# A GRU scan on one core: 1 - z moves from ScalarE to VectorE, the order of VectorE's step changes, and the scan's transfers go out once per tile

## The chip, the core and the metric

The kernel runs on one core of a Trainium2 chip (trn2). The metric is the device time of one execution in microseconds (us). A core has TensorE (PE, with its weight loads shown as PEld), VectorE (DVE), ScalarE (ACT), GpSimd (POOL) and SyncE (SP), which here only issues transfers. Each engine runs its own instructions strictly in the order in which they are written and waits for the others through semaphores.

## The reference

Inputs are x (16 x 256 x 512), a condition vector per batch (16 x 512), and weights. Two residual layers follow each other:

```
x = x + L0(x, cond)    # RMS norm, scale and shift from cond, 16-head attention over 256 positions, o + o @ W_out
x = x + L1(cond, x)    # GRU over the 256 positions; the first state is cond

# L1, one step, for each position in turn:
gi = x @ W_ih + b_ih ; gh = h @ W_hh + b_hh          # each 16 x 1536, split in r, z, n
r = sigmoid(i_r + h_r) ; z = sigmoid(i_z + h_z)
n = tanh(i_n + r * h_n)
h = (1 - z) * n + z * h                              # output of this position, state of the next
```

## The kernel before

The program has two stages. The first, up to about 772 us, computes the attention layer and the first two tiles of gi. The change does not touch it. The second is the scan: 256 steps, one after the other, since each needs the state h of the step before. A tile is ST = 8 steps, so there are 32 tiles.

The state h (16 x 512) is kept as 128 partitions x 128 columns: partition group j (32 partitions, 16 of them used) holds columns 128 j to 128 j + 127 of h. Every step is cut in two halves, q = 0 and q = 1, of 64 of these 128 columns. A half of a step is this chain, named by the functions of the code:

- TensorE multiplies the turned state hT by W_hh (line 632) into PSUM bank q, in which the gi part of the step already lies. The work of a step is 8 groups of 4 multiplications in the order (q, c) = (0,0), (0,1), (1,0), (0,2), (0,3), (1,1), (1,2), (1,3), with c a quarter of the sum over h. The profile counts two MATMUL rows for each, so a group is 8 rows and a step 64. Group (0,0) waits until half 0 of the new state is turned, (1,0) until bank 1 holds its gi part, and (0,2) until half 1 of the new state is turned, as c = 0 and 1 need half 0 of hT and c = 2 and 3 half 1.
- gates(q), line 1067, ACT: tanh for r and z once all four groups of half q are there. The kernel writes a sigmoid as (1 + tanh(a/2))/2.
- r_times_n(q), line 865, DVE: needs gates(q). Then before_n(q), line 870, DVE, and tanh_n(q), line 1075, ACT.
- one_less_z(q), line 1071, ACT: 1 - z out of gates(q). z_times_h(q), line 874, DVE: z times the old state. Both are needed after tanh_n(q).
- new_part(q), line 880, DVE: needs tanh_n(q). new_h(q), line 884, DVE. turn_h(q), line 891, DVE: the 32 x 32 block transpose that makes hT for the next step.
- seed(q), line 1084, ACT: copies the gi part of the next step into PSUM bank q.

Behind the multiplications of a step TensorE runs 4 or 5 of the 36 pieces (line 604, 128 x 512 columns each) that compute gi of a tile two tiles ahead; `START` spreads them evenly over steps 0 to 239, so 120 steps have 4, 120 have 5, and the last 16 have none. Once per tile, 29 times in steps 0 to 239 and each time in a step of 4 pieces, TensorE also turns a block of x (line 502). The results pass through nat (line 738, DVE) into DRAM (gscr, line 288) and come back laid out for the scan in a buffer GI (lines 277 and 282), two of which alternate. POOL adds the residual (line 1184, s_og counts steps) into outG, which SP stores (line 360). SP walks through the steps as well: before the change it waits for s_og at each step and issues one to three of the transfers.

Of the kernel before, what the change touches and what calls it, by code (L numbers as in the profile page):

```python
# [8 lines left out]
ALU = mybir.AluOpType  # L9
ACT = mybir.ActivationFunctionType  # L10
# [8 lines left out]
ST = 8  # L19
NT = T // ST  # L20
# [51 lines left out]
def cond_resid_kernel(nc, x, cond, W_emb, b_emb, g_norm, W_qkv, g_q, g_k, W_out, W_ih, W_hh, b_ih, b_hh, out):  # L72
# [3 lines left out]
    with ExitStack() as ctx:  # L76
# [29 lines left out]
        bias = sb("bias", [128, 3 * D])  # L106
# [67 lines left out]
        GI = [GI0, GI1]  # L174
# [67 lines left out]
        def _(sp):  # L242
# [27 lines left out]

            def gi_free(tt):

                sp.wait_ge(s_og, ST * (tt - 1))
                sp.wait_ge(s_h, 2 * ST * (tt - 1))

            def load_gx(tt, j):
                sp.dma_start(GI[tt % 2][32 * j:32 * j + 16, :, 4, :], x_j[tt, j]).then_inc(s_gl[tt % 2], 16)

            def load_gates(tt, j):
                v = gscr[tt].rearrange("(s b) j g f -> j b s (g f)", s=ST)  # L280
                sp.wait_ge(s_st[tt % 2], 48 * (tt // 2 + 1))
                sp.dma_start(GI[tt % 2][32 * j:32 * j + 16, :, 1:4, :].rearrange("p s g f -> p s (g f)"),
                             v[j]).then_inc(s_gl[tt % 2], 16)

# [52 lines left out]
            load_x1(1)  # L337
            sp.wait_ge(s_bz, 9)
            for j in range(4):
                load_gx(0, j)  # L340
            load_x1(2)
            store_x1(NB - 1, 1)
            for g in range(3):
                store_gate(0, g)
            for j in range(4):
                load_gates(0, j)
            load_x1(3)
            for g in range(3):
                store_gate(1, g)
            sp.wait_ge(s_bz, 17)  # L350
            for j in range(4):
                load_gx(1, j)
                load_gates(1, j)
            load_x1(4)

            o_v = out.rearrange("b (t s) (j f) -> t j b s f", s=ST, j=4)

            def store_h(tt, j):
                sp.wait_ge(s_og, ST * (tt + 1))
                sp.dma_start(o_v[tt, j], outG[32 * j:32 * j + 16, tt % 2, :, :]).then_inc(s_out[tt % 2], 16)  # L360

            for t in range(T):
                tt, s = t // ST, t % ST

                if tt:
                    sp.wait_ge(s_og, t)
                    if s < 4:
                        store_h(tt - 1, s)
                    if tt + 1 < NT:
                        if s == 0:  # L370
                            gi_free(tt + 1)
                        if s < 2:
                            load_gx(tt + 1, 2 * s)
                            load_gx(tt + 1, 2 * s + 1)
                        elif s < 6:
                            load_gates(tt + 1, s - 2)
                for pt, g, k, turn in pieces(t):
                    if turn and pt + 3 < NT:
                        load_x1(pt + 3)
                    if k == GP - 1:  # L380
                        store_gate(pt, g)
            for j in range(4):
                store_h(NT - 1, j)
            for e in range(2):
# [258 lines left out]
        def _(v):  # L643
# [214 lines left out]
            for t in range(T):  # L858
# [4 lines left out]
                def r_times_n(q):  # L863
                    v.wait_ge(s_tr, 2 * t + q + 1)
                    v.scalar_tensor_tensor(out=v_v[:, q, :], in0=v_rz[:, q, 0:64], scalar=1.0, in1=ps[:, q, 0:64],  # L865
                                           op0=ALU.add, op1=ALU.mult).then_inc(s_u, 1)

                def before_n(q):
                    v.wait_ge(s_u, 2 * t + q + 1)
                    v.scalar_tensor_tensor(out=v_w[:, q, :], in0=v_v[:, q, :], scalar=0.5, in1=gi[:, f[q]],  # L870
                                           op0=ALU.mult, op1=ALU.add).then_inc(s_w, 1)

                def z_times_h(q):
                    v.scalar_tensor_tensor(out=v_h[:, q, :], in0=v_rz[:, q, 64:128], scalar=1.0, in1=h_old[:, f[q]],
                                           op0=ALU.add, op1=ALU.mult)

                def new_part(q):

                    v.wait_ge(s_n, 2 * t + q + 1)
                    v.tensor_tensor(v_n[:, q, :], v_n[:, q, :], v_c[:, q, :], ALU.mult).then_inc(s_d, 1)  # L880
# [11 lines left out]

                r_times_n(0)
                before_n(0)
                if t >= 2:
                    v.wait_ge(s_og, t - 1)
                z_times_h(0)
                new_part(0)
                r_times_n(1)
                new_h(0)  # L900
                before_n(1)
                turn_h(0)
                z_times_h(1)
# [10 lines left out]
        def _(s):  # L914
# [149 lines left out]
            for t in range(T):  # L1064
# [3 lines left out]

                def one_less_z(q):
                    s.wait_ge(s_tr, 2 * t + q + 1)  # L1070
                    s.activation(v_c[:, q, :], v_rz[:, q, 64:128], ACT.Copy, bias=0.5, scale=-0.5)  # L1071

                def tanh_n(q):
# [13 lines left out]
                gates(0)  # L1087
                one_less_z(0)
                tanh_n(0)
                gates(1)  # L1090
                seed(0)
                one_less_z(1)
                tanh_n(1)
# [119 lines left out]
```

## Time and profile before

| | us |
|---|---|
| median of 3 runs (lowest, highest) | 1822.72 (1821.93, 1822.9) |
| the profiled execution: its own time | 1821.93 |
| its span, first to last instruction | 1820.1 |
| PE busy | 1755.0 (96%) |
| DVE busy | 1191.0 (65%) |
| ACT busy | 1008.7 (55%) |
| POOL busy | 409.4 (22%) |

Some 1.8 us of the profiled execution lie outside the span. The share of busy time is a mean over both stages and does not say which engine sets the time of a step; the rows of single steps do. In such rows the first number is the start in us from the span's start, the second the duration, and a number in brackets is how long the engine had been idle.

### The profile page before, as it was taken

The page shows a single profiled execution, that of the slowest core. Times are in us where ns is not written, and L with a number is a line of the kernel's source. Part 1 is how long each engine was busy: PE and PEld are TensorE (multiplying, and loading weights), DVE is VectorE, ACT ScalarE, POOL GpSimd, SP SyncE. Part 2 cuts the span into 40 slices and gives each one's busy share as a digit, 9 for nine tenths or more (in the row PEclk, how much of TensorE's full clock was granted, in tenths as well). Part 3 has the DMA queues.
Part 4 walks back from the last instruction along what each step waited for, and adds up shares of the span by engine and source line. Part 5 has one row for each costly group of instructions (what it writes and reads, how often), then busy time and mean ns, then how long its engine had stood idle before and what let it go on. Part 6 is the DMA issues. An engine that isn't in the chain of part 4 may idle for free.

```text
span 1820.1 us, 59314 instructions
## 1 busy us (share of the span) xinstructions
PE 1755.0 (96%) x23849; PEld 1293.7 (71%) x23849; DVE 1191.0 (65%) x4508; ACT 1008.7 (55%) x3691; POOL 409.4 (22%) x481
## 2 busy tenths in 40 slices
PE   6999999999999998799999999999999999999986
PEld 4677777777777776577777777777777777777765
DVE  5777777777777777355666666666665666666554
ACT  4777777777777776144444444444444444444444
POOL 5533333333433432111111111111111111111111
PEclk8999999999999999899999999999999999999999
DMA  5021111111111111743332332323323233232220
GB/s 214 23 96 42 42 36 36 36 36 36 36 36 36 36 36 35 157 71 75 78 79 70 75 75 76 79 72 73 76 76 76 74 72 77 74 78 69 64 68 14
DMA packets 130490, 118.80 MB, mean 65 GB/s; under 512 B 9932, under 2 KB 108440, under 8 KB 130216
## 3 DMA queue, kind: packets, MB, share of 16 engines
q1 hardware_dynamic: 130216, 115.00, 24.1%
q8 instruction: 190, 3.11, 0.8%
q14 instruction: 84, 0.69, 0.1%
HBM read 73.01 MB, written 41.94 MB: 63 GB/s over the span
## 4 chain that ended last, share of the span: by engine, by line
PE 93%; DMA 2%; ACT 2%; DVE 1%; issue 1%; POOL 1%; SPq 0%; POOLq 0%; DVEq 0%
PE ps L632 38%; PE ps L604 17%; PE ps L422 13%; PE ps L461 7%; PE ps L492 5%; PE ps L448 4%; PE ps L475 4%; PE ps L430 2%; PE ps L404 1%; PE ps L502 1%; PE ps L482 1%; DMA xscr<-x1s 1%; ACT qT L955 1%; ACT P L969 0%; DMA wemb<-in_L_cond_W_emb_dram 0%
## 5 line engine op out<-in xcount | busy, mean ns | idle before, releaser
L632 PE MATMUL ps<-whh,hT 128*32 128x192 f32 x16384 | 719.0, 327 | 20.9 <-DVE hT L891 17.4
L632 PEld LDWEIGHTS ps<-whh,hT 128*32 128x32 f32 x16384 | 546.4, 110 | 194.2 <-issue 84.9
L1067 ACT ACTIVATE v<-ps 128x128 f32<-128x128 f32 x512 | 139.1, 272 | 441.5 <-PE ps L632 441.5
L1184 POOL TENSOR_TENSOR outG<-hG,GI 128x128 f32<-128x128 f32 x256 | 117.1, 457 | 959.9 <-DVE hG L884 959.9
L865 DVE SCALAR_TENSOR_TENSOR v<-v,ps 128x64 f32<-128x64 f32 x512 | 113.4, 222 | 316.6 <-ACT v L1067 316.6
L969 ACT ACTIVATE P<-ps,nmx 128x256 f32<-128x256 f32 x512 | 242.4, 489 | 0.7 <-DVE nmx L690 0.7
L1075 ACT ACTIVATE v<-v 128x64 f32<-128x64 f32 x512 | 131.4, 257 | 107.1 <-DVE v L870 107.1
L1123 POOL TENSOR_TENSOR rq<-msq,mh 128x16 f32<-128x16 f32 x64 | 187.1, 2923 | 5.3
L690 DVE TENSOR_REDUCE nmx<-ps 128x2 f32<-128x512 f32 x256 | 164.9, 686 | 29.8 <-PE ps L448 28.0
L422 PE MATMUL ps<-wqh,xh 128*128 128x512 f32 x384 | 165.5, 431 | 4.7 <-POOL xl L1114 4.6
L604 PE MATMUL ps<-wih_h,x1h 128*128 128x512 f32 x384 | 166.6, 434 | 1.4 <-DVE x1l L729 1.4
L604 PE MATMUL ps<-wih_h,x1l 128*128 128x512 f32 x384 | 164.3, 428 | 0.0
L1084 ACT COPY ps<-GI 128x192 f32<-128x192 f32 x510 | 163.2, 320 | 0.0
L880 DVE TENSOR_TENSOR v<-v,v 128x64 f32<-128x64 f32 x512 | 115.5, 226 | 63.7 <-ACT v L1075 47.9
L422 PE MATMUL ps<-wql,xh 128*128 128x512 f32 x384 | 152.9, 398 | 0.0
L422 PE MATMUL ps<-wqh,xl 128*128 128x512 f32 x384 | 151.4, 394 | 0.0
L604 PE MATMUL ps<-wih_l,x1h 128*128 128x512 f32 x384 | 151.4, 394 | 0.0
L1034 ACT COPY PT<-ps 128x512 f32<-128x512 f32 x128 | 75.1, 586 | 125.8 <-PE ps L461 125.7
L461 PE MATMUL ps<-ident,P 128*128 128x128 f32 x1024 | 140.3, 280 | 1.8 <-DVE rTs L695 1.3
L461 PEld LDWEIGHTS ps<-ident,P 128*128 128x128 f32 x1024 | 109.8, 141 | 44.7 <-issue 42.1
L1071 ACT ACTIVATE v<-v 128x64 f32<-128x64 f32 x512 | 130.7, 255 | 8.1
L891 DVE STREAM_TRANSPOSE hT<-hG 128x64 f32<-128x64 f32 x510 | 123.4, 242 | 8.8
(104 smaller groups left out, 2449.3 us busy)
## 6 DMA issues: line engine op xcount, KB each, us to landing
gscr<-nat SPq DMA_DIRECT2D x96, 256.0 KB, 2.6
GI<-gscr SPq DMA_DIRECT2D x128, 192.0 KB, 3.7
xb<-in_x_dram SPq DMA_DIRECT2D x16, 512.0 KB, 3.7
xres<-in_x_dram SPq DMA_DIRECT2D x32, 256.0 KB, 2.8
xscr<-x1s SPq DMA_DIRECT2D x32, 256.0 KB, 2.0
x1n<-xscr SPq DMA_DIRECT2D x32, 256.0 KB, 2.7
GI<-xscr SPq DMA_DIRECT2D x128, 64.0 KB, 2.7
out_dram<-outG SPq DMA_DIRECT2D x128, 64.0 KB, 2.9
```

The lines of the kernel that those rows point to most:

```text
L422: last = pe.matmul(pB, xp[:, c, m], wp[:, c, n], start=(c == 0 and k == 0), stop=(c == KC - 1 and k == 2))
L461: last = pe.transpose(pP[:, j, k, :], P[:, U % 2, j, 128 * k:128 * k + 128], ident)
L604: last = pe.matmul(F[G % 2], xp[:, tt % 2, c, :], wp[:, c, g * D:(g + 1) * D], start=(k == 0), stop=(k == GP - 1), skip_group_check=True)
L632: last = pe.matmul(ps[32 * j:32 * j + 32, q, 0:192], hT[:, 32 * c:32 * c + 32], whg[:, c, :, 128 * j + 64 * q:128 * j + 64 * q + 64], star ...
L690: v.tensor_reduce(nmx[:, U % 2, 2 * h:2 * h + 2], pS2[h], AXX, ALU.max, negate=True).then_inc(s_mx, 1)
L891: v.transpose(hT[:, f[q]], h_new[:, f[q]]).then_inc(s_hc, 1)
L969: last = s.activation(P[:, U % 2, j, :], pS[j], ACT.Exp, bias=nmx[:, U % 2, j:j + 1], accum_out=rsum[:, U % 2, j:j + 1])
L1067: s.activation(v_rz[:, q, :], ps[:, q, 64:192], ACT.Tanh, scale=0.5).then_inc(s_tr, 1)
L1071: s.activation(v_c[:, q, :], v_rz[:, q, 64:128], ACT.Copy, bias=0.5, scale=-0.5)
L1075: s.activation(v_n[:, q, :], v_w[:, q, :], ACT.Tanh).then_inc(s_n, 1)
L1084: s.copy(ps[:, q, 0:192].rearrange("p (g f) -> p g f", g=3), GI[(t + 1) // ST % 2][:, (t + 1) % ST, 0:3, 64 * q:64 * q + 64]).then_inc(s_s ...
L1123: g_.tensor_tensor(rq[:, i, :], msq[:, i, :], mh, ALU.pow).then_inc(s_rq, 1)
```

## The change

Three things change.

- one_less_z(q) leaves ACT (an activation with scale and bias) and becomes a tensor_scalar on DVE. ACT's wait in front of it goes with it.
- The order of DVE's step changes. Before: r_times_n(1) stands between new_part(0) and new_h(0), and before_n(1) ahead of turn_h(0). After: new_h(0) stands ahead of r_times_n(1), turn_h(0) follows, and one_less_z(1) and before_n(1) come behind turn_h(0). The wait for s_og (POOL's residual of two steps ago) moves from z_times_h(0) to one_less_z(0).
- SP no longer waits for s_og at every step. At the last step of a tile it waits once, issues the four stores of the tile at once, and behind them the four loads of x and the four of the gates for the tile two further on.

The core of the diff, DVE and ACT:

```diff
+                def one_less_z(q):
+                    v.tensor_scalar(v_c[:, q, :], v_rz[:, q, 64:128], -0.5, 0.5, ALU.mult, ALU.add)
...
                 r_times_n(0)
-                before_n(0)
                 if t >= 2:
                     v.wait_ge(s_og, t - 1)
+                one_less_z(0)
+                before_n(0)
                 z_times_h(0)
                 new_part(0)
+                new_h(0)
                 r_times_n(1)
-                new_h(0)
+                turn_h(0)
+                one_less_z(1)
                 before_n(1)
-                turn_h(0)
                 z_times_h(1)
                 new_part(1)
                 new_h(1)
...
-                def one_less_z(q):
-                    s.wait_ge(s_tr, 2 * t + q + 1)
-                    s.activation(v_c[:, q, :], v_rz[:, q, 64:128], ACT.Copy, bias=0.5, scale=-0.5)
...
                 gates(0)
-                one_less_z(0)
                 tanh_n(0)
                 gates(1)
                 seed(0)
-                one_less_z(1)
                 tanh_n(1)
                 seed(1)
```

SP:

```diff
+            def load_gx(tt):
+                x1_there(tt)
+                sp.wait_ge(s_bz, (9, 17)[tt % 2])
+                if tt >= 2:
+                    sp.wait_ge(s_og, ST * (tt - 1))
+                    sp.wait_ge(s_h, 2 * ST * (tt - 1))
+                for j in range(4):
+                    sp.dma_start(GI[tt % 2][32 * j:32 * j + 16, :, 4, :], x_j[tt, j]).then_inc(s_gl[tt % 2], 16)
+
+            def load_g(tt):
                 v = gscr[tt].rearrange("(s b) j g f -> j b s (g f)", s=ST)
+                if tt:
+                    load_gx(tt)
                 sp.wait_ge(s_st[tt % 2], 48 * (tt // 2 + 1))
-                sp.dma_start(GI[tt % 2][32 * j:32 * j + 16, :, 1:4, :].rearrange("p s g f -> p s (g f)"),
-                             v[j]).then_inc(s_gl[tt % 2], 16)
+                for j in range(4):
+                    sp.dma_start(GI[tt % 2][32 * j:32 * j + 16, :, 1:4, :].rearrange("p s g f -> p s (g f)"),
+                                 v[j]).then_inc(s_gl[tt % 2], 16)
...
-                if tt:
-                    sp.wait_ge(s_og, t)
-                    if s < 4:
-                        store_h(tt - 1, s)
-                    if tt + 1 < NT:
-                        if s == 0:
-                            gi_free(tt + 1)
-                        if s < 2:
-                            load_gx(tt + 1, 2 * s)
-                            load_gx(tt + 1, 2 * s + 1)
-                        elif s < 6:
-                            load_gates(tt + 1, s - 2)
                 for pt, g, k, turn in pieces(t):
                     if turn and pt + 3 < NT:
                         load_x1(pt + 3)
                     if k == GP - 1:
                         store_gate(pt, g)
+                        if g == 2:
+                            stored = pt
+                            if t > ST * (pt - 1) - 1:
+                                load_g(pt)
+                if s == ST - 1:
+                    sp.wait_ge(s_og, t + 1)
+                    for j in range(4):
+                        sp.dma_start(o_v[tt, j], outG[32 * j:32 * j + 16, tt % 2, :, :]).then_inc(s_out[tt % 2], 16)
+                    if tt + 2 <= stored:
+                        load_g(tt + 2)
```

The instructions as they stand in the built programs follow. Line numbers of the changed program are its own: there r_times_n is L854, one_less_z L858, before_n L862, z_times_h L866, new_part L871, new_h L875 and turn_h L882. In the names v_113 is the buffer of tanh(r) and tanh(z), v_114 of r times n, v_115 of tanh_n's input, v_116 of n, v_117 of 1 - z and v_118 of z times h.

DVE in the scan, one whole step of the kernel before, from r_times_n(0) to turn_h(1):

```order
L865 SCALAR_TENSOR_TENSOR v_114<-v_113,ps 128x64
L870 SCALAR_TENSOR_TENSOR v_115<-v_114,GI_104 128x64
L874 SCALAR_TENSOR_TENSOR v_118<-v_113,hG 128x64
L880 TENSOR_TENSOR v_116<-v_116,v_117 128x64
L865 SCALAR_TENSOR_TENSOR v_114<-v_113,ps 128x64
L884 SCALAR_TENSOR_TENSOR hG<-v_118,v_116 128x64
L870 SCALAR_TENSOR_TENSOR v_115<-v_114,GI_104 128x64
L891 STREAM_TRANSPOSE hT<-hG 128x64
L874 SCALAR_TENSOR_TENSOR v_118<-v_113,hG 128x64
L880 TENSOR_TENSOR v_116<-v_116,v_117 128x64
L884 SCALAR_TENSOR_TENSOR hG<-v_118,v_116 128x64
L891 STREAM_TRANSPOSE hT<-hG 128x64
```

DVE, the first 12 of the 14 instructions of one step of the changed kernel, from r_times_n(0) to new_part(1) (new_h(1) and turn_h(1) follow):

```order
L854 SCALAR_TENSOR_TENSOR v_114<-v_113,ps 128x64
L858 TENSOR_SCALAR v_117<-v_113 128x64
L862 SCALAR_TENSOR_TENSOR v_115<-v_114,GI_107 128x64
L866 SCALAR_TENSOR_TENSOR v_118<-v_113,hG 128x64
L871 TENSOR_TENSOR v_116<-v_116,v_117 128x64
L875 SCALAR_TENSOR_TENSOR hG<-v_118,v_116 128x64
L854 SCALAR_TENSOR_TENSOR v_114<-v_113,ps 128x64
L882 STREAM_TRANSPOSE hT<-hG 128x64
L858 TENSOR_SCALAR v_117<-v_113 128x64
L862 SCALAR_TENSOR_TENSOR v_115<-v_114,GI_107 128x64
L866 SCALAR_TENSOR_TENSOR v_118<-v_113,hG 128x64
L871 TENSOR_TENSOR v_116<-v_116,v_117 128x64
```

The second SCALAR_TENSOR_TENSOR that reads ps, r_times_n(1), has moved from ahead of new_h(0) to behind it, and between it and before_n(1) now stand the transpose and the TENSOR_SCALAR.

ACT in one step of the kernel before (L1067 gates, L1071 one_less_z, L1075 tanh_n, L1084 seed), from gates(0) to seed(1):

```order
L1067 ACTIVATE v_113<-ps 128x128
L1071 ACTIVATE v_117<-v_113 128x64
L1075 ACTIVATE v_116<-v_115 128x64
L1067 ACTIVATE v_113<-ps 128x128
L1084 COPY ps<-GI_104 128x192
L1071 ACTIVATE v_117<-v_113 128x64
L1075 ACTIVATE v_116<-v_115 128x64
L1084 COPY ps<-GI_104 128x192
```

ACT in one step of the changed kernel (L1060 gates, L1064 tanh_n, L1073 seed):

```order
L1060 ACTIVATE v_113<-ps 128x128
L1064 ACTIVATE v_116<-v_115 128x64
L1060 ACTIVATE v_113<-ps 128x128
L1073 COPY ps<-GI_104 128x192
L1064 ACTIVATE v_116<-v_115 128x64
L1073 COPY ps<-GI_104 128x192
```

The two ACTIVATE into v_117 are gone and the rest keeps its order.

SP in the scan of the kernel before, from the store of one gate of a tile to the loads of the next tile's GI (L288 gscr, L269 x, L360 output, L277 and L282 GI):

```order
L269 DMA x1n_105<-xscr 128x512
L288 DMA gscr<-nat_111 512x1x128
L360 DMA out_dram<-outG 16x8x128
L277 DMA GI_107<-xscr 16x8x128 x2
L360 DMA out_dram<-outG 16x8x128
L277 DMA GI_107<-xscr 16x8x128 x2
L360 DMA out_dram<-outG 16x8x128
L282 DMA GI_107<-gscr 16x8x384
L288 DMA gscr<-nat_110 512x1x128
L360 DMA out_dram<-outG 16x8x128
```

SP of the changed kernel (L292 gscr, L269 x, L370 output, L278 and L286 GI), from one tile's gate loads to the next tile's:

```order
L269 DMA x1n_121<-xscr 128x512
L292 DMA gscr<-nat_110 512x1x128
L370 DMA out_dram<-outG 16x8x128 x4
L278 DMA GI_104<-xscr 16x8x128 x4
L286 DMA GI_104<-gscr 16x8x384 x4
L292 DMA gscr<-nat_111 512x1x128 x2
L269 DMA x1n_105<-xscr 128x512
```

Transfers that stood one or two at a time between stores of the gates now stand as a block of 4, 4 and 4 once per tile.

## Rows read from the trace of the kernel before

**Rows 1.** Stretches: us, PE, PEld, DVE, ACT, POOL busy, granted clock, DMA share, GB/s

```profile
1500.00:1752.00 252.00, 251.07 (x4267) 182.06 (x4263) 154.87 (x775) 118.00 (x503) 28.18 (x62) 1.00 0.29 72
1755.00:1811.00 56.00, 39.59 (x904) 33.35 (x908) 31.21 (x172) 26.08 (x114) 6.39 (x14) 1.00 0.14 30
```

**Rows 2.** Timeline (start, duration, engine, line, operation), the first step's r_times_n(0)

```profile
774.91 0.22 DVE L865 SCALAR_TENSOR_TENSOR v<-v,ps 128x64 f32<-128x64 f32 x1 [2.94 <-ACT v L1067]
```

**Rows 3.** Timeline, r_times_n(0) of the last step

```profile
1812.91 0.22 DVE L865 SCALAR_TENSOR_TENSOR v<-v,ps 128x64 f32<-128x64 f32 x1 [1.41 <-ACT v L1067]
```

**Rows 4.** Waits from 1755 to 1811 us: total, times, longest

```profile
PE ps L632 <- DVE hT L891: 17.4, 15, 1.2
```

**Rows 5.** Timeline of one step without pieces (last: idle before, releaser)

```profile
1769.30 0.22 DVE L865 SCALAR_TENSOR_TENSOR v<-v,ps 128x64 f32<-128x64 f32 x1 [1.42 <-ACT v L1067]
...
1769.55 0.23 DVE L870 SCALAR_TENSOR_TENSOR v<-v,GI 128x64 f32<-128x64 f32 x1
1769.69 0.22 DVE L874 SCALAR_TENSOR_TENSOR v<-v,hG 128x64 f32<-128x64 f32 x1
...
1770.10 0.23 DVE L880 TENSOR_TENSOR v<-v,v 128x64 f32<-128x64 f32 x1 [0.19 <-ACT v L1075]
...
1770.27 0.22 DVE L865 SCALAR_TENSOR_TENSOR v<-v,ps 128x64 f32<-128x64 f32 x1
1770.38 0.25 ACT L1071 ACTIVATE v<-v 128x64 f32<-128x64 f32 x1
1770.41 0.22 DVE L884 SCALAR_TENSOR_TENSOR hG<-v,v 128x64 f32<-128x64 f32 x1
1770.54 0.22 DVE L870 SCALAR_TENSOR_TENSOR v<-v,GI 128x64 f32<-128x64 f32 x1
1770.68 0.24 DVE L891 STREAM_TRANSPOSE hT<-hG 128x64 f32<-128x64 f32 x1
1770.84 0.18 DVE L874 SCALAR_TENSOR_TENSOR v<-v,hG 128x64 f32<-128x64 f32 x1
1770.96 0.31 ACT L1084 COPY ps<-GI 128x192 f32<-128x192 f32 x1
...
1771.06 0.37 PE L632 MATMUL ps<-whh,hT 128*32 128x192 f32 x4 [1.16 <-DVE hT L891]
```

**Rows 6.** Timeline, a step with 5 pieces

```profile
1203.19 0.22 DVE L865 SCALAR_TENSOR_TENSOR v<-v,ps 128x64 f32<-128x64 f32 x1 [1.41 <-ACT v L1067]
...
1205.09 2.81 PE L632 MATMUL ps<-whh,hT 128*32 128x192 f32 x64
```

**Rows 7.** The page's groups: count, busy us, mean ns, idle before

```profile
L632 PE MATMUL ps<-whh,hT 128*32 128x192 f32 x16384 | 719.0, 327 | 20.9 <-DVE hT L891 17.4
```

**Rows 8.** Timeline, the step that also turns a block of x

```profile
1027.76 0.22 DVE L865 SCALAR_TENSOR_TENSOR v<-v,ps 128x64 f32<-128x64 f32 x1 [0.97 <-ACT v L1067]
...
1029.86 2.32 PE L632 MATMUL ps<-whh,hT 128*32 128x192 f32 x52
```

**Rows 9.** Timeline, DVE's end of the step of rows 5

```profile
1771.08 0.23 DVE L880 TENSOR_TENSOR v<-v,v 128x64 f32<-128x64 f32 x1
1771.34 0.22 DVE L884 SCALAR_TENSOR_TENSOR hG<-v,v 128x64 f32<-128x64 f32 x1
1771.60 0.24 DVE L891 STREAM_TRANSPOSE hT<-hG 128x64 f32<-128x64 f32 x1
```

**Rows 10.** One line's instructions: count, duration ns min/median/max, starts

```profile
L759 DVE TENSOR_SCALAR gqs<-vT x1: 144/144/144, 16.8 to 16.8; 128x1 f32<-128x1 f32 x1
```

**Rows 11.** Another line's instructions, columns as in rows 10

```profile
L647 DVE TENSOR_SCALAR xb<-xb,rx x32: 476/479/486, 13.0 to 645.3; 128x512 f32<-128x512 f32 x32
```

**Rows 12.** SP's timeline, the loads of one tile's GI

```profile
1199.65 0.88 SPq L277 DMA_DIRECT2D GI<-xscr  x2
...
1212.66 5.87 SPq L282 DMA_DIRECT2D GI<-gscr  x3
```

**Rows 13.** Chain of waits at the scan's start: start, us, what

```profile
764.53 7.28 DMA GI<-gscr
```

More of the change, by code:

```diff
@@ L269, in load_x1 @@
                 sp.dma_start(x1n[tt % 2], x_v[tt]).then_inc(s_xl[tt % 2], 16)
[L271 to L279, printed above, removed]
+            def load_gx(tt):
[7 more added lines that the diff above has]
+            def load_g(tt):
                 v = gscr[tt].rearrange("(s b) j g f -> j b s (g f)", s=ST)
+                if tt:
+                    load_gx(tt)
                 sp.wait_ge(s_st[tt % 2], 48 * (tt // 2 + 1))
-                sp.dma_start(GI[tt % 2][32 * j:32 * j + 16, :, 1:4, :].rearrange("p s g f -> p s (g f)"),
-                             v[j]).then_inc(s_gl[tt % 2], 16)
+                for j in range(4):
+                    sp.dma_start(GI[tt % 2][32 * j:32 * j + 16, :, 1:4, :].rearrange("p s g f -> p s (g f)"),
+                                 v[j]).then_inc(s_gl[tt % 2], 16)
             def store_gate(tt, g):
@@ L337, in _ @@
             load_x1(1)
-            sp.wait_ge(s_bz, 9)
-            for j in range(4):
-                load_gx(0, j)
+            load_gx(0)
             load_x1(2)
@@ L344, in _ @@
                 store_gate(0, g)
-            for j in range(4):
-                load_gates(0, j)
+            load_g(0)
             load_x1(3)
@@ L349, in _ @@
                 store_gate(1, g)
[L350 to L353, printed above, removed]
+            load_g(1)
             load_x1(4)
             o_v = out.rearrange("b (t s) (j f) -> t j b s f", s=ST, j=4)
-            def store_h(tt, j):
-                sp.wait_ge(s_og, ST * (tt + 1))
-                sp.dma_start(o_v[tt, j], outG[32 * j:32 * j + 16, tt % 2, :, :]).then_inc(s_out[tt % 2], 16)
+            stored = 0
             for t in range(T):
                 tt, s = t // ST, t % ST
-                if tt:
-                    sp.wait_ge(s_og, t)
-                    if s < 4:
-                        store_h(tt - 1, s)
-                    if tt + 1 < NT:
-                        if s == 0:
-                            gi_free(tt + 1)
-                        if s < 2:
-                            load_gx(tt + 1, 2 * s)
-                            load_gx(tt + 1, 2 * s + 1)
-                        elif s < 6:
-                            load_gates(tt + 1, s - 2)
                 for pt, g, k, turn in pieces(t):
@@ L381, in _ @@
                         store_gate(pt, g)
-            for j in range(4):
-                store_h(NT - 1, j)
+                        if g == 2:
[8 more added lines that the diff above has]
+                        load_g(tt + 2)
             for e in range(2):
```

## The prediction, as it was made before the changed kernel had run

> **What bounds the kernel now.** The busy shares point at TensorE (96% of the span), and a busy TensorE is easily taken for the limit. So I went first to the table of stretches: from 1500 to 1752 us, while TensorE also works on gi, it is busy 251.07 of 252 us; from 1755 to 1811 us, without that work, 39.59 of 56 us, at the same granted clock of 1.00 (the 2.4 GHz level) [rows 1]. Next I wanted the length of a step in both. I measure it from r_times_n(0) to r_times_n(0), and call that moment of each step 0. Over the whole scan it is (1812.91 - 774.91) / 255 = 4.071 us [rows 2, 3]. In the bare steps the waits say what ends last: TensorE waits 15 times for turn_h, 17.4 us in all, so 1.16 each [rows 4]. The timeline of one such step [rows 5] shows turn_h(0) starting at 1.38 (1770.68 - 1769.30) and TensorE's group (0,0) at 1.76.
>
> How long is a bare step? The group spacing follows from the merged row of 64 multiplications in 2.81 us [rows 6]: one of them runs 0.33 us [rows 7], and a half group (four at once) takes half the spacing, so with s the spacing 2.81 = 8 s - s/2 + 0.33, and s = 0.33 us. That puts (0,2) three groups behind (0,0): 1.76 + 0.98 = 2.74. The bare step is 17.4 / 15 = 1.16 us of waiting plus the 2.81 us run = 3.97 us, so the next 0 comes 3.97 - 2.74 = 1.23 behind the start of (0,2). With a piece count of 5, (0,0) starts at 1205.09 - 1203.19 = 1.90 [rows 6] and in the 29 steps that also turn a block of x at 1029.86 - 1027.76 = 2.10 [rows 8]: by the same 2.21 from (0,0) to the next 0 these take 4.11 and 4.31 us. The sum closes: 1038.0 less 120 x 4.11 and 29 x 4.31 leaves 419.8 for the other 106 intervals, 3.96 each, the bare step's length, so the steps of 4 pieces are set by the chain of the state too. So TensorE's own work costs at most 0.34 us over the bare chain of half 0, and the chain of the state is almost as long as TensorE's work everywhere.
>
> The number that matters most is the slack of half 1. turn_h(1) starts at 1771.60 - 1769.30 = 2.30 [rows 9], and TensorE starts 0.38 after a transpose starts (1770.68 to 1771.06, [rows 5]): hT is ready for (0,2) at 2.68. It is wanted at 2.74. Half 1 is late if it loses more than 0.06 us in a bare step, 0.20 in one of 5 pieces and 0.40 in the turning one.
>
> **The order on VectorE, step by step.** All from [rows 5, 9]. A dependent instruction starts 0.25 to 0.26 behind its predecessor's start (L865 to L870, L880 to L884, L884 to L891), an independent one 0.13 to 0.14 behind it (L870 to L874, L865 to L884, L884 to L870), and one behind the transpose 0.16. From before_n to new_part, with tanh_n on ScalarE between, it is 0.55 in half 0 and 0.54 in half 1. What the rows do not have is the new TENSOR_SCALAR on 64 columns. From above, its slot is that of L874, 0.14, or at the far end the 0.22 of a whole such record, as if nothing overlapped. From below, 0, as if the engine took no turn for it. I take 0.11: a TENSOR_SCALAR of one column took 144 ns [rows 10] and one of 512 columns 479 [rows 11], which by a straight line makes 144 + 63/511 x 335 = 185 ns for 64, about 0.04 less than the 0.22 us of the two-input ones, so 0.14 - 0.04 = 0.10, and I round up.
>
> The Trainium skill's "VectorE: DVE Perf Modes", section "The perf-mode tier table (the rule you actually need)", says that a tensor_scalar from SBUF to SBUF runs fp32 at two elements a cycle while a tensor_tensor stays at one. By it the slot would be an estimated 0.14 - 32/960 = 0.107 us, and the sum the same; no row here has this form at this size.
>
> Half 0 after: r_times_n(0) 0; one_less_z(0) 0.14; before_n(0) at 0.25 (0.14 + 0.11, and it waits until 0.25 anyway, so nothing is lost); new_part(0) 0.80; new_h(0) 1.06, where r_times_n(1) no longer stands ahead of it; r_times_n(1) 1.19; turn_h(0) 1.33. Half 0 gains 0.05: group (0,0) could start at 1.71 instead of 1.76.
>
> Half 1 after: r_times_n(1) 1.19, against 0.97 before (1770.27), since it now stands behind new_h(0), and its engine waits there for tanh_n(0). Then it has to let two more pass: the transpose at 1.33, one_less_z(1) at 1.49, before_n(1) at 1.60 (before 1.24, so 0.36 later); new_part(1) 2.14; new_h(1) 2.40; turn_h(1) 2.66. hT is ready at 2.66 + 0.38 = 3.04, where the old schedule wants it at 2.74. The next 0 comes at 3.04 + 1.23 = 4.27 us.
>
> The other edits on the path: seed(1) starts 0.42 and ends 0.73 behind before_n(1) [rows 5], so at 2.33. With the 0.14 that TensorE also needs behind a transpose's end (0.38 less its 0.24) that is 2.47 for (1,0), wanted at 1.71 + 0.65 = 2.36 at the earliest. (0,2) would follow at 2.80, before 3.04, so the 0.11 vanishes in the wait for half 1. What ScalarE no longer does cost nothing: one_less_z(1) began at 1770.38 and filled a pause before tanh_n(1), which waits for before_n(1) [rows 5]. If VectorE is delayed, no engine gains from a free ScalarE. The wait for s_og asks for POOL's work of two steps ago and moves 0.28 us ahead: over 3 us in hand, price 0. Behind turn_h(1) VectorE has in some steps the copy of a gate or of x, 512 columns as those of [rows 11]; were it even 1 us from 2.82, it would end at 3.82, before 4.27.
>
> SP: the block of 12 transfers has to land before seed(0) of the tile's last step, 7 steps later, about 29 us. The loads of one tile now begin at 1199.65 and the last three are issued over 5.87 us from 1212.66 [rows 12], so they are out at 1218.5. In a block, at 0.43 us (L277, 0.88 for two) to 1.96 us each (5.87 / 3), 12 take 5 to 24 us, and the last lands up to 7.28 later, as where four went out together [rows 13]: 12 to 31 us. The upper end is 12 times the worst issue, which also contained waiting for a step; I take 12 to 15, hidden behind the tile, price 0.
>
> **Sum.** In every step but the 29 turning ones half 1 sets 4.27; those keep TensorE's 4.31 (their (0,2) is at 2.10 + 0.98 = 3.08, behind 3.04). 226 x 4.27 + 29 x 4.31 = 1090.0, less the 1038.0 of now: +52.0. The last step ends with new_h(1) 0.35 later. Profiled execution 1821.93 + 52.4 = 1874.3; the median of the runs shown lies 0.8 above it: 1875 us, 2.9% slower. The slot of the TENSOR_SCALAR hits half 1 whole and half 0 by what goes over 0.11. At 0.14: 0.03 + 0.03 (with rounding 4.33), 255 x 4.33 - 1038 = +66, 1889. At 0.22: 4.49, +107, 1930. At 0, half 1 sets 4.16, less than TensorE's 4.31 in the 29: 226 x 4.16 + 29 x 4.31 - 1038 = +27, 1850.
>
> **Rivals.**
> 1. The TENSOR_SCALAR takes a full slot of 0.14 to 0.16: 1889 to 1899. For it: L874 next to it on the same engine takes 0.14. Against: [rows 10, 11]. 20%.
> 2. Not slower: half 0 alone sets the step, as the waits of the bare steps now say (TensorE waits for the transpose ahead of (0,0)). Then the 0.05 of half 0 comes through where TensorE's pieces do not bind, in the 106 intervals that the chain sets now: -5 us, 1817. It holds only if turn_h(1) starts by 2.74 - 0.38 = 2.36, and I have 2.66. For it speaks that TensorE wants half 1 later where pieces delay (0,0); but in the steps of 5 pieces the slack is 0.20 against a delay of 0.36. 3%, and 1% that the two cancel.
> 3. Each VectorE instruction waits for the end of the one ahead, so that instructions added between cost their whole record. With 0.22 or 0.24 for each independent one: before_n(0) 0.41, new_part(0) 0.96, new_h(0) 1.22, r_times_n(1) 1.44, turn_h(0) 1.66, one_less_z(1) 1.90, before_n(1) 2.09, turn_h(1) 3.15, next 0 at 4.76: +176, 1998. The rows are against it [rows 5]: L884 starts 0.14 behind L865, whose record is 0.22. 1%. The Trainium skill's "VectorE: DVE Perf Modes", section "The DRAIN you can't avoid", gives such a rule, that the next op does not start until the pipe is empty, and lets one that is not held start earlier; the rows side with the exception.
> 4. The block of transfers lands late, beyond 29 us after its start: seed(0) of the last step of 30 tiles would wait. At the 31 us of the upper bound that is 2 us x 30 = 60 on top, 1935. 3%.
> 5. Half 1 loses less than worked out (a smaller slot, or a shorter way from transpose to (0,2) with TensorE already running): 1850 to 1862. 7%.
>
> **How the numbers follow.** The forecast with its near surroundings, 1862 to 1886, has 65%; rivals 1 to 5 the rest. Reaching to 1862 below and 1897 above leaves out rivals 2 to 5 and the last 2% of rival 1: 17%. Within 0.2% (3.6 us, about what a measurement of this kernel can tell from no change): 2%; faster 3%; slower 95%.
>
> **What would show it.** In the changed profile a bare and a 5-piece step should have the same length, 4.27. The waits of TensorE should name turn_h in nearly every step, not 15 times, at about 0.2 to 0.3 us between (1,0) and (0,2), and TensorE's busy share should fall. From r_times_n(0): r_times_n(1) 1.19, before_n(1) 1.60, turn_h(1) 2.66. The slot behind the TENSOR_SCALAR tells rival 1 (0.14). A loaded GI that ends late would show as ACT waiting for a DMA at seed(0) once per tile. I am wrong if turn_h(1) still starts by 2.36, or if TensorE waits at (1,0) for seed(1) longer than at (0,2).

## The result, and the profile after

The changed kernel takes 1854.86 us (median of 4 runs, 1852.87 to 1855.4), against 1822.33 before in the same comparison: ratio 1.0176, 95% interval 1.0158 to 1.0194. It is slower, as forecast, but by 32.5 us and not by 52. The forecast of 1875 and its range from 1862 both lie too high. The profiled execution was the longest of all, 1860.83 us with a span of 1859.0, so the step lengths below are read from it and the total from the timed runs.

Here is one bare step (without pieces) near the end of the scan, in the VectorE timeline of the changed kernel (start, duration, line, operation, idle before; L854 r_times_n, L858 one_less_z, L862 before_n, L866 z_times_h, L871 new_part, L875 new_h, L882 turn_h). It answers to [rows 5, 9].

```profile
1847.53 0.22 DVE L854 SCALAR_TENSOR_TENSOR v<-v,ps 128x64 f32<-128x64 f32 x1 [1.29 <-ACT v L1060]
1847.66 0.19 DVE L858 TENSOR_SCALAR v<-v 128x64 f32<-128x64 f32 x1
1847.78 0.23 DVE L862 SCALAR_TENSOR_TENSOR v<-v,GI 128x64 f32<-128x64 f32 x1
...
1848.33 0.23 DVE L871 TENSOR_TENSOR v<-v,v 128x64 f32<-128x64 f32 x1 [0.19 <-ACT v L1064]
1848.59 0.22 DVE L875 SCALAR_TENSOR_TENSOR hG<-v,v 128x64 f32<-128x64 f32 x1
1848.73 0.21 DVE L854 SCALAR_TENSOR_TENSOR v<-v,ps 128x64 f32<-128x64 f32 x1
1848.86 0.24 DVE L882 STREAM_TRANSPOSE hT<-hG 128x64 f32<-128x64 f32 x1
1849.02 0.15 DVE L858 TENSOR_SCALAR v<-v 128x64 f32<-128x64 f32 x1
1849.09 0.22 DVE L862 SCALAR_TENSOR_TENSOR v<-v,GI 128x64 f32<-128x64 f32 x1
...
1850.15 0.24 DVE L882 STREAM_TRANSPOSE hT<-hG 128x64 f32<-128x64 f32 x1
1851.68 0.22 DVE L854 SCALAR_TENSOR_TENSOR v<-v,ps 128x64 f32<-128x64 f32 x1 [1.29 <-ACT v L1060]
```

With 1847.53 as 0: r_times_n(1) at 1.20 (forecast 1.19), turn_h(0) 1.33 (1.33), one_less_z(1) 1.49 (1.49), before_n(1) 1.56 (1.60), turn_h(1) 2.62 (2.66), and the next step at 4.15 (4.27). VectorE's order did what was said of it. The step of 4.15 instead of 4.27 is not what was said.

TensorE's rows of the same stretch show the two places at which it waits:

```profile
1849.22 0.84 PEld L621 LDWEIGHTS ps<-whh,hT 128*32 128x32 f32 x24 [1.47 <-ACT ps L1073]
1849.25 3.04 PE L621 MATMUL ps<-whh,hT 128*32 128x192 f32 x64 [1.12 <-DVE hT L882]
...
1850.45 1.46 PEld L621 LDWEIGHTS ps<-whh,hT 128*32 128x32 f32 x40 [0.39 <-DVE hT L882]
```

The weight loads of hT stop after 24, that is behind group (1,0), and go on at 1850.45, released by turn_h(1). That is the wait at (0,2) of the forecast. But it ends 0.30 us behind the start of turn_h(1) (1850.15), while group (0,0), at 1849.22 and 1849.25, starts 0.36 to 0.39 behind turn_h(0) (1848.86). Over the whole scan the weight loads wait for turn_h 218 times, once in nearly every step; before, only the 15 waits ahead of (0,0) in [rows 4] name it. The list (total us, times, longest):

```profile
PEld ps L621 <- issue: 92.7, 247, 2.2
PEld ps L593 <- issue: 75.3, 240, 2.4
PEld ps L621 <- DVE hT L882: 66.9, 218, 0.4
...
PE ps L621 <- DVE hT L882: 16.8, 15, 1.1
PE ps L621 <- issue: 3.4, 4, 1.8
```

The last numbers of the first two lines, 2.2 and 2.4 us, are new: before, TensorE's loads never waited longer than 0.5 us on "issue". By the starts of gates(0) in the trace, steps of 4 pieces, of 5 and bare ones take 4.15 us alike, the turning ones 4.30, and seven steps, all the fourth of their tile (step 3, from 0), take 4.54 to 8.00. TensorE in the stretch before one of them and in it:

```profile
1021.56 3.03 PE L621 MATMUL ps<-whh,hT 128*32 128x192 f32 x64
1026.64 0.50 PE L593 MATMUL ps<-wih_h,x1l 128*128 128x512 f32 x1 [2.05 <-issue]
...
1027.69 0.40 PE L593 MATMUL ps<-wih_l,x1h 128*128 128x512 f32 x1
1028.02 4.49 PE L621 MATMUL ps<-whh,hT 128*32 128x192 f32 x64
```

Two things happen. TensorE stands idle for 2.05 us ahead of a piece that waits for nothing. Then the next 64 multiplications take 4.49 us, where those of the step ahead took 3.03, their wait for half 1 included. The second is the clock, as two stretches show (columns as in [rows 1]; behind POOL's share stands the granted clock):

```profile
1024.60:1028.20 3.60, 1.56 (x9) 1.02 (x13) 1.78 (x11) 1.03 (x5) 0.46 (x1) 1.00 0.25 74
1028.30:1031.60 3.30, 3.30 (x48) 2.18 (x44) 0.00 (x0) 0.28 (x1) 0.00 (x0) 0.50 0.00 0
```

After the idle stretch the granted clock falls from 1.00 (2.4 GHz) to 0.50 (1.2 GHz), and it is back at 1.00 in the stretch from 1031.70. It fell in the two longest of the seven steps, 7.62 and 8.00 us, and in none of the other five. Together the seven are 11.0 us longer than seven steps of 4.15; 7.3 us of that lie in these two. What the transfers did meanwhile, from 1011.5 to 1023.5 us (the DMA line is the busy share of the 16 engines in 40 slices, in tenths; then queue, kind, packets, MB, share):

```profile
DMA  0199987779876645376899999999999999999961
...
q1 hardware_dynamic: 2255, 1.57, 85.6%
```

and in the kernel before, in a stretch at the same time of the same length:

```profile
q8 instruction: 2, 0.03, 1.3%
```

The program's own instructions are loaded by the DMA engines too, as packets of the queues q8 and q14. Those of q8 are TensorE's. Each has 16 KB, and in the scan of either kernel 35406 records of TensorE stand against 138 packets, 256.6 to a packet. The page of before and that of the changed kernel both count 190 packets of q8, though VectorE has 512 instructions more and ScalarE 512 fewer; e5 below, with 255 records more on TensorE alone, has 191, and e8, with 210 fewer, 189.

Before, two packets of q8 pass in these 12 us. In the changed kernel not one does, while the block of SP keeps the engines 85.6% busy. Over the scan behind 790 us the packets of q8 start at most 9.2 us apart in the kernel before; in the changed one 13 of the gaps are 10.1 to 13.3 us. Every long step shows the same: TensorE stops at the same place in a block of 256 of its records (189 to 193 past a multiple of 256, counted from the program's start) and goes on 1.3 to 1.5 us after the late packet of q8 has landed. Here the packet takes 1.67 us from 1023.57, and TensorE goes on at 1026.64. So TensorE had no instructions to run.

### The profile page after: what moved, and what is told of

Read it like the earlier page. It is cut to its first block, busy times and chain, and to the rows that moved or that the text cites. A ratio compares the mean times of both kernels' runs of the same rounds, so it can differ in the third digit from the quotient of the medians.

```text
span 1859.0 us, 59130 instructions
## 1 busy us (share of the span) xinstructions
PE 1790.1 (96%) x23849; PEld 1238.9 (67%) x23849; DVE 1237.4 (67%) x5020; ACT 896.2 (48%) x3179; POOL 407.0 (22%) x481
## 4 chain that ended last, share of the span: by engine, by line
PE 93%; DMA 2%; ACT 2%; DVE 2%; issue 1%; POOL 1%; SPq 0%; POOLq 0%; DVEq 0%
PE ps L621 39%; PE ps L593 16%; PE ps L411 13%; PE ps L450 7%; PE ps L481 5%; PE ps L437 4%; PE ps L464 4%; PE ps L419 2%; PE ps L393 1%; PE ps L491 1%; PE ps L471 1%; DMA xscr<-x1s 1%; ACT qT L948 1%; ACT P L962 0%; DMA wemb<-in_L_cond_W_emb_dram 0%
## 5 line engine op out<-in xcount | busy, mean ns | idle before, releaser
L621 PE MATMUL ps<-whh,hT 128*32 128x192 f32 x16384 | 752.8, 329 | 22.9 <-DVE hT L882 16.8
L621 PEld LDWEIGHTS ps<-whh,hT 128*32 128x32 f32 x16384 | 488.4, 110 | 286.9 <-issue 92.7
L1060 ACT ACTIVATE v<-ps 128x128 f32<-128x128 f32 x512 | 139.5, 272 | 401.0 <-PE ps L621 401.0
L854 DVE SCALAR_TENSOR_TENSOR v<-v,ps 128x64 f32<-128x64 f32 x512 | 111.0, 217 | 275.8 <-ACT v L1060 275.8
L1064 ACT ACTIVATE v<-v 128x64 f32<-128x64 f32 x512 | 131.2, 256 | 305.0 <-DVE v L862 305.0
L871 DVE TENSOR_TENSOR v<-v,v 128x64 f32<-128x64 f32 x512 | 115.1, 225 | 95.8 <-ACT v L1064 95.8
L1073 ACT COPY ps<-GI 128x192 f32<-128x192 f32 x510 | 162.9, 319 | 0.0
L882 DVE STREAM_TRANSPOSE hT<-hG 128x64 f32<-128x64 f32 x510 | 122.9, 241 | 8.8
L875 DVE SCALAR_TENSOR_TENSOR hG<-v,v 128x64 f32<-128x64 f32 x512 | 115.2, 225 | 17.6
```

What stands on the lines that cost most here:

```text
L621: last = pe.matmul(ps[32 * j:32 * j + 32, q, 0:192], hT[:, 32 * c:32 * c + 32], whg[:, c, :, 128 * j + 64 * q:128 * j + 64 * q + 64], star ...
L882: v.transpose(hT[:, f[q]], h_new[:, f[q]]).then_inc(s_hc, 1)
L1060: s.activation(v_rz[:, q, :], ps[:, q, 64:192], ACT.Tanh, scale=0.5).then_inc(s_tr, 1)
L1064: s.activation(v_n[:, q, :], v_w[:, q, :], ACT.Tanh).then_inc(s_n, 1)
L1073: s.copy(ps[:, q, 0:192].rearrange("p (g f) -> p g f", g=3), GI[(t + 1) // ST % 2][:, (t + 1) % ST, 0:3, 64 * q:64 * q + 64]).then_inc(s_s ...
```

## The experiments

In all of them the total length of the scan is read from the first and the last start of gates in one line's rows (L1067 of before). The row of before, from the scan's stretch (count, duration ns min/median/max, first and last start):

```profile
L1067 ACT ACTIVATE v<-ps x512: 262/273/278, 774.6 to 1813.6; 128x128 f32<-128x128 f32 x171
```

The same of e2, explained below:

```profile
L1071 ACT ACTIVATE v<-ps x512: 264/272/278, 775.6 to 1839.9; 128x128 f32<-128x128 f32 x171
```

Of e3:

```profile
L1066 ACT ACTIVATE v<-ps x512: 258/272/278, 778.6 to 1837.7; 128x128 f32<-128x128 f32 x171
```

Of e5:

```profile
L1072 ACT ACTIVATE v<-ps x512: 262/277/280, 776.8 to 1863.9; 128x128 f32<-128x128 f32 x171
```

Of e8:

```profile
L1070 ACT ACTIVATE v<-ps x512: 262/273/278, 775.9 to 1809.5; 128x128 f32<-128x128 f32 x171
```

So the scan takes 1039.0 us before, and 1064.3, 1059.1, 1087.1 and 1033.6 us in these four; the other lengths of the table come from the same row of each trace.

| | median us (runs) | ratio, 95% interval | scan us | steps of 4 pieces, 5, turning |
|---|---|---|---|---|
| before | 1822.8, 1822.6 (11, 11) | | 1039.0 | 3.97, 4.10, 4.30 |
| changed | 1854.86 (4) | 1.0176 [1.0158, 1.0194] | 1075.7 | 4.15, 4.15, 4.30, and 7 long |
| e1 SP alone | 1834.49 (5) | 1.0059 [1.0047, 1.0072] | 1053.2 | 3.97, 4.10, 4.31, and 9 long |
| e2 VectorE and ScalarE alone | 1849.57 (5) | 1.0148 [1.0135, 1.0161] | 1064.3 | 4.15, 4.15, 4.29 |
| e3 order alone | 1842.95 (4) | 1.0113 [1.01, 1.0127] | 1059.1 | 4.13, 4.13, 4.30 |
| e4 one_less_z alone | 1833.24 (5) | 1.0058 [1.0046, 1.007] | 1049.2 | 4.07, 4.10, 4.31 |
| e5 second wait at (0,2) | 1868.47 (5) | 1.0249 [1.0235, 1.0263] | 1087.1 | 4.24, 4.24, 4.31, and 1 long |
| e6 block one step later | 1826.56 (6) | 1.0029 [1.0017, 1.004] | 1045.6 | 3.97, 4.10, 4.31, and 4 long |
| e7 order, wait for s_og as before | 1830.64 (5) | 1.0046 [1.0033, 1.0058] | 1047.0 | 4.06, 4.10, 4.30 |
| e8 wait for seed(0) moved | 1817.07 (6) | 0.9971 [0.996, 0.9983] | 1033.6 | 3.89, 4.10, 4.30 |

The step lengths are medians over the starts of gates(0) in each trace; "long" are steps above 4.5 us. The one long step of e5, and one each in e1 and e6, is step 2 of the first tile. e5 has no block; there the loads with which the scan begins keep the DMA engines 82.9% busy from 772 to 790 us (78.9% in the kernel before, which has no long step there). In all 21 long steps of the table TensorE stops at the same place of a block of 256 records and goes on 1.2 to 1.5 us after a packet of q8 has landed.

**e1, SP's part alone.** The kernel before with the changed SP program, no other edit:

```diff
-                if tt:
-                    sp.wait_ge(s_og, t)
...
+                if s == ST - 1:
+                    sp.wait_ge(s_og, t + 1)
...
+                    if tt + 2 <= stored:
+                        load_g(tt + 2)
```

> The kernel before with SP's part of the change alone: the block of 4 stores and 8 loads once per tile. My forecast priced it at 0. Theory A (the block delays TensorE's instruction loading): no step gets longer by a constant amount, but in some tiles the step about three behind the tile's start lasts 0.4 to 4 us longer, with TensorE idle for no cause but its own issue; 2 to 11 us in all, so 1824 to 1833, and executions differ among themselves by several us. Theory B (the forecast: transfers are hidden, and the long steps of the changed kernel come from its later schedule): 1822, and all steps as before. Theory C (late landing of the loads): ScalarE waits for a load at seed(0) of step 7 of a tile, not TensorE at step 3.

It cost 11.7 us (1834.49 against 1822.83), a little above what theory A had, and its runs spread over 6.7 us (1830.52 to 1837.21). Its ordinary steps are those of before to 0.01 us. Nine steps are long, seven of them step 3 of a tile, the longest 8.25 us; in the two longest (8.10 and 8.25 us) the granted clock also falls to 0.50. TensorE stands idle on issue, as in this row of TensorE's timeline in tile 4:

```profile
924.08 2.79 PE L621 MATMUL ps<-whh,hT 128*32 128x192 f32 x60 [0.76 <-issue]
```

So the block is not free, and neither the new schedule nor a late landing (theory C, a wait at step 7) makes the long steps.

**e2, VectorE and ScalarE alone.** The changed kernel with SP's functions and loop of before.

> The changed kernel with SP's transfers as they were before: the part on VectorE and ScalarE alone. Theory A: 226 steps of 4.15 and 29 of 4.30, none longer: (226 x 4.15 + 29 x 4.30) - 1038.0 = +24.6, and 0.3 at the end, so 1847 (1845 to 1849), steady within 0.1%. Theory B (the long steps belong to the new schedule): 1851 to 1857 with steps of 5 to 8 us as in the changed kernel.

Steps of 4.15, 4.15 and 4.29 us and not one longer: the scan is 25.3 us longer than before, where theory A had 24.6. The median of 1849.57 is 2.6 us above its 1847; in the profiled execution the stage ahead of the scan is 1.0 us longer, which the edit does not touch, and the kernel before itself spreads over 1820.05 to 1825.36 in 22 runs. I leave that at noise.

**e3, the order alone.** e2, with one_less_z back on ScalarE:

```diff
                 if t >= 2:
                     v.wait_ge(s_og, t - 1)
-                one_less_z(0)
                 before_n(0)
...
                 turn_h(0)
-                one_less_z(1)
                 before_n(1)
```

> VectorE's new order alone: new_h(0) ahead of r_times_n(1), turn_h(0) ahead of before_n(1); one_less_z stays on ScalarE, the transfers as before. Theory 1 (half 1 sets the step, and TensorE wakes 0.30 behind the start of turn_h(1), as the changed kernel's profile shows): before_n(1) at 1.33 + 0.16 = 1.49, turn_h(1) 2.55, next step at 2.55 + 0.30 + 1.23 = 4.08 us in the 106 intervals that took 3.97, while those of 5 pieces stay at 4.11 and the turning ones at 4.30: +12, 1834 (1831 to 1837). Theory 2 (it is the TENSOR_SCALAR that costs, the order is free): 1822. Theory 3 (waking takes 0.38 as the forecast had it): 4.16 and 1844.

4.13 us, between theory 1 (4.08) and theory 3 (4.16): all three missed. VectorE's timeline of e3 shows why: r_times_n(0), then before_n(0).

```profile
1816.30 0.22 DVE L865 SCALAR_TENSOR_TENSOR v<-v,ps 128x64 f32<-128x64 f32 x1 [1.29 <-ACT v L1066]
1816.63 0.22 DVE L870 SCALAR_TENSOR_TENSOR v<-v,GI 128x64 f32<-128x64 f32 x1
```

before_n(0) starts 0.33 behind it, where it was 0.25 in [rows 5]. With one_less_z(0) gone, the wait for s_og had fallen to before_n(0), which already waits for r_times_n(0). The residual of two steps ago that it asks for had long been added, and the wait cost 0.07 us all the same. The trace has the reason. Of two waits at one instruction, one becomes an instruction of its own, a record EVENT_SEMAPHORE ahead of it: e3 has 254 of them on VectorE at before_n(0), e2 and e7 none. It is this extra instruction that waits for r_times_n(0), the wait that ends last; it starts 0.26 us behind r_times_n(0), and before_n(0) follows 0.07 us later. That was my experiment's own fault, and e7 undoes it.

**e7, the order alone, clean.** e3 with the wait back where it was:

```diff
-                if t >= 2:
-                    v.wait_ge(s_og, t - 1)
                 before_n(0)
+                if t >= 2:
+                    v.wait_ge(s_og, t - 1)
                 z_times_h(0)
```

> VectorE's new order alone as in e3, but with the wait for s_og at z_times_h(0) as before, where e3 had it at before_n(0) beside another wait, and before_n(0) began at 0.32 instead of 0.26. Theory 1 (that second wait cost 0.07 us of half 0 and so of the step): before_n(1) at 1.49, turn_h(1) 2.52, the step 2.52 + 0.30 + 1.23 = 4.05 to 4.06 in the 106 intervals of 3.97, the others at TensorE's 4.10 and 4.30: +9, 1832 (1830 to 1834). Theory 2 (the wait's place is free): 4.12 as in e3 and 1841.

4.06 us and 1830.64: theory 1. The order by itself costs 8 us. Against e2 the TENSOR_SCALAR then costs 0.10 us in each step (4.153 less 4.055), though its slot behind the transpose is 0.07; the rest is before_n(1), whose record is 0.18 us directly behind the transpose and 0.21 behind the TENSOR_SCALAR.

**e4, one_less_z alone.** VectorE's order of before, with the TENSOR_SCALAR ahead of before_n; the wait for s_og moves to one_less_z(0), as in the changed kernel:

```diff
-                before_n(0)
                 if t >= 2:
                     v.wait_ge(s_og, t - 1)
+                one_less_z(0)
+                before_n(0)
                 z_times_h(0)
                 new_part(0)
                 r_times_n(1)
                 new_h(0)
+                one_less_z(1)
                 before_n(1)
                 turn_h(0)
```

> one_less_z(q) on VectorE directly ahead of before_n(q), the order otherwise as before, transfers as before. Theory 1 (every instruction ahead of turn_h(0) and before_n(1) costs its slot, 0.07 us for this one by the changed kernel's profile; in half 0 it is covered by the wait for r_times_n): turn_h(0) and the next group (0,0) 0.07 later, 4.04 us in the 106 intervals of 3.97, the others under TensorE's cover: +7, 1830 (1827 to 1832). Theory 2 (all of the loss is in the order): 1822. Theory 3 (a slot of 0.14): 4.11 in the 106, +15, 1837.

4.07 us in the steps of 4 pieces, 0.10 more than before where theory 1 had 0.07 and theory 3 0.14; the scan is 10.2 us longer, the median 10.4. The order is not all of the loss. Between new_h(0) and before_n(1) the slot is 0.10 here, as these rows of VectorE's timeline in e4 show (L886 new_h(0), L869 one_less_z(1), L873 before_n(1), L893 turn_h(0)):

```profile
1805.51 0.22 DVE L886 SCALAR_TENSOR_TENSOR hG<-v,v 128x64 f32<-128x64 f32 x1
1805.65 0.18 DVE L869 TENSOR_SCALAR v<-v 128x64 f32<-128x64 f32 x1
1805.75 0.21 DVE L873 SCALAR_TENSOR_TENSOR v<-v,GI 128x64 f32<-128x64 f32 x1
1805.89 0.23 DVE L893 STREAM_TRANSPOSE hT<-hG 128x64 f32<-128x64 f32 x1
```

So half 0 bears it, turn_h(0) and with it group (0,0) 0.10 later, and ScalarE's relief gives nothing back.

**e5, a second wait at group (0,2).** On e2:

```diff
                     elif (q, c) == (0, 2) and t:
+                        pe.wait_ge(s_sd, 2 * t)
                         pe.wait_ge(s_hc, 2 * t + 1)
```

> The changed VectorE and ScalarE part with the transfers as before (the kernel of e2), and at TensorE's group (0,2) a second wait, for seed(1), which has long been met there. It asks why hT woke TensorE 0.30 us behind the start of turn_h(1) where I had taken 0.38 from group (0,0), which waits for two semaphores. Theory 1 (a second wait on an instruction costs some 0.06 us, even if met, once it stands behind the one that comes last or as a piece of its own): the 226 steps go from 4.15 to 4.21, so +13 on e2's scan. Theory 2 (TensorE wakes more slowly after a long pause, whatever it waits for): 4.15 as in e2.

The steps grow from 4.15 to 4.24, by 0.084 us before rounding, and the median to 1868.47. Theory 1, and more than its 0.06. The rows are turn_h(1) and the weight loads that it releases, first in the timeline of e2:

```profile
1821.12 0.24 DVE L893 STREAM_TRANSPOSE hT<-hG 128x64 f32<-128x64 f32 x1
1821.42 0.48 PEld L632 LDWEIGHTS ps<-whh,hT 128*32 128x32 f32 x16 [0.39 <-DVE hT L893]
```

Then in the timeline of e5:

```profile
1844.71 0.25 DVE L894 STREAM_TRANSPOSE hT<-hG 128x64 f32<-128x64 f32 x1
1845.07 0.19 PEld L633 LDWEIGHTS ps<-whh,hT 128*32 128x32 f32 x8 [0.46 <-issue]
```

The weight load starts 0.30 behind turn_h(1) with one wait and 0.36 with two, as at (0,0), and the first multiplication 0.30 and 0.39, although the added semaphore had been met already (seed(1) ends before (1,0) starts, which waits for it too). As in e3, the second wait is a record EVENT_SEMAPHORE of its own: TensorE has 373 of them in the scan of e2 and 628 in that of e5. In e5 the wait for hT, the late one, sits on the extra instruction at (0,2), as it does at (0,0) in the kernel before: that instruction starts 0.28 to 0.29 us behind the transpose's start, and the weight load follows 0.08 later. In the code it is the wait written last, here and in e3. Whether the cost goes when the two are written the other way round was not tried.

**e6, the block later.** e1, with the block behind POOL's residual of the next tile's first step:

```diff
+            def block_of(tt):
+                sp.wait_ge(s_og, min(ST * (tt + 1) + 1, T))
...
+                if tt and s == 1:
+                    block_of(tt - 1)
```

> The kernel before with the block of 12 transfers once per tile, as in e1, but issued one or two steps later (it waits for POOL's residual of the next tile's first step). Theory A (the block holds up TensorE's instruction loading while it runs): the long steps move with the block, from step 3 of a tile to step 4 or 5, and cost about the same, 5 to 15 us. Theory B (step 3 is long for what is done in it, for instance the store of a gate): they stay at step 3.

Apart from one in the first tile, the long steps are now step 4 of tiles 11, 14 and 25. They have moved with the block, by the one step by which it starts later. The block costs less here, 1826.56, and in the profile three tiles are hit where the changed kernel had seven. Over 10 us lie between two packets of q8 14 times here as well, but at most 12.5 us, where e1 has up to 13.1.

**e8, one wait fewer at group (0,0).** The kernel before, with the wait for seed(0) at the last piece of the step ahead:

```diff
-                        if t:
+                        if t and not waited[t - 1]:
                             pe.wait_ge(s_sd, 2 * t - 1)
...
+                    if waited[t] and (3 * pt + g - 6) * GP + k == START[t + 1] - 1:
+                        pe.wait_ge(s_sd, 2 * t + 1)
                     gate_piece(pt, g, k)
```

> The kernel before, with one edit on TensorE: where the step before has pieces of gi, the wait for seed(0) stands at the last of them (unless that one has waits of its own) and group (0,0) waits for hT alone. Theory 1 (the second wait costs about 0.06 us where hT comes last): the steps of 4 pieces fall from 3.97 to 3.91, those of 5 stay at 4.10, so -5 us, 1817 (1816 to 1819). Theory 2 (waking is slower after a pause of any kind, not by the number of waits): 1822, no change.

Theory 1: the steps of 4 pieces fall to 3.89 (forecast 3.91), those of 5 and the turning ones stay under TensorE's own work. The bare steps, where the edit leaves the second wait in place, keep their 3.97. The kernel takes 1817.07 us, ratio 0.9971 with an interval of 0.996 to 0.9983. It beats both kernels. turn_h(0) and the loads behind it in one such step, from the timeline of e8; they start 0.29 behind it, though TensorE had pieces until then:

```profile
1702.32 0.24 DVE L894 STREAM_TRANSPOSE hT<-hG 128x64 f32<-128x64 f32 x1
1702.61 2.43 PEld L633 LDWEIGHTS ps<-whh,hT 128*32 128x32 f32 x64 [0.27 <-DVE hT L894]
```

## Why the prediction was right and where it was wrong

**The order on VectorE: right.** That half 1 takes over, because r_times_n(1) stands behind new_h(0) and before_n(1) behind two more, holds to 0.01 us for r_times_n(1), turn_h(0) and one_less_z(1). e7 shows that the order alone makes the steps longer, and e4 that ScalarE's relief gives nothing back.

**The slot of the TENSOR_SCALAR: nearly right.** I took 0.11. It is 0.10 between two-input instructions (e4) but 0.07 behind the transpose, where it counted in the changed kernel. That is 0.04 us a step, 226 x 0.04 = 9 us too much. In the sum it is the smaller of the two terms that were mis-sized. Rival 1 (a full slot of 0.14) is out.

**"TensorE starts 0.38 after a transpose starts": the step that failed.** I read it at group (0,0) and used it at (0,2), also for the slack of half 1. Group (0,0) waits for two semaphores and (0,2) for one, which starts it 0.08 us sooner (e5, e8): at (0,0) the wait for hT sits on an extra instruction ahead of the weight load, at (0,2) on the load itself. 226 x 0.08 = 18 us too much, so 0.30 and not 0.38 was the term to use. With 0.30 and the measured 2.62, the forecast's own sum gives 2.62 + 0.30 + 1.23 = 4.15, the measured step. The two mis-sized terms together are 226 x 0.12 = 27 us, and 1875 - 27 = 1848, where e2, which is this part alone, has 1849.57. The slack of half 1 in the kernel before was 0.14 us by this, and not 0.06; the forecast loss of 0.36 was far over both.

**The turning steps: right.** Forecast 4.31, measured 4.30.

**"SP: price 0": wrong in kind.** I asked only whether the loads land in time, and they do (rival 4 is out). What the block delays are TensorE's own instructions, and after the longest stops the lower clock adds to the loss; the forecast had neither. By the runs it costs 5.3 us on top of e2 (1854.86 against 1849.57, from two comparisons) and 11.7 us on top of the kernel before. That it cost less in the longer steps is measured; why is open. It was luck that this unpriced term went against the other two: without it the forecast would have been 25 us too high and not 20.

**The other rivals.** Rival 2 (half 0 alone sets the step) is out by e7. Rival 3, by which nothing overlaps on VectorE, is out: slots of 0.07 and 0.10 stand beside records of 0.15 and 0.18. The rule in the Trainium skill's "VectorE: DVE Perf Modes", section "The DRAIN you can't avoid", that the next op does not start until the pipe is empty, does not fit these slots; its exception, that an op which is not held starts earlier, does. Rival 5, a smaller slot or a shorter way to (0,2), was what happened, with 7% and a range of 1850 to 1862 of its own (the VectorE part alone, at 1849.57, lies just under it); its reason, that TensorE is already running, is not the one: in e5 TensorE runs as in e2 and starts late all the same. I named it and did not look for what would separate the two groups, which the code shows.

That TensorE lacked instructions rests on four things: the idle time at instructions that wait for nothing, no packet of q8 while the block ran, the move of the long steps in e6, and the place at which TensorE stops and goes on in all 21 long steps. A run with fewer instructions to load was not made.

## What to carry to other kernels

When a wait moves from one instruction to another, take the time from the signal to the start from an instruction with as many waits as the new one has. Put a wait that was met long ago on an instruction that has no other wait and that nobody is waiting for: that made e8 5.6 us faster than before. On an engine that works in order, the price of an edit is the slots in front of the instruction that feeds the other engine, and a saving on an engine that has pauses is worth nothing. Before bundling transfers, ask not only whether they land in time but what else the DMA engines carry meanwhile. Here TensorE's instructions came by them all through the scan, a packet about every 8 us, and gaps of 11 to 13 us between two of them stopped it in some tiles.

## What the runs showed of the hardware

- A second wait at one instruction is an instruction of its own ahead of it (EVENT_SEMAPHORE, 255 more on TensorE in e5 than in e2, 254 on VectorE in e3), and in these runs the late wait sat on it. It cost 0.08 us a step on TensorE (e5, e8) and 0.07 us on VectorE (e3 against e7), though the other semaphore had been reached long before.
- TensorE's instructions came as packets of 16 KB of queue q8, one for 256 of its records. A block of 12 transfers that kept the DMA engines 85.6% busy for 12 us let none through, and TensorE was without instructions for up to 2.4 us at a time, in 7 of 30 tiles of the profiled execution of the changed kernel.
- After the two longest of these stops in the changed kernel the granted clock was 0.50 (1.2 GHz) for a stretch, and 64 multiplications took 4.49 us where the step ahead had 3.03.
- Behind a TENSOR_SCALAR of 64 columns VectorE started the next instruction after 0.07 us when the TENSOR_SCALAR itself stood behind a transpose (changed kernel) and after 0.10 us when it stood behind new_h(0) (e4); behind the two-input forms it was 0.13 to 0.14 us ([rows 5]).
